# Layer 3's attention: probabilities turned in 32x32 blocks by VectorE, values weighted in 32x32 tiles of TensorE, and the steps of layers 2 and 3 ordered anew

## What is computed

```python
q = (x @ Wq + bq).reshape(b, l, KVH, GROUPS, HD).transpose(0, 2, 3, 1, 4)   # KVH 8, GROUPS 4, HD 16
k = (ctx @ Wk + bk).reshape(b, s, KVH, HD).transpose(0, 2, 1, 3)
v = (ctx @ Wv + bv).reshape(b, s, KVH, HD).transpose(0, 2, 1, 3)
attn = softmax(einsum('bkgld,bksd->bkgls', q, k) / 4 + mask)
out = einsum('bkgls,bksd->bkgld', attn, v).transpose(0, 3, 1, 2, 4).reshape(b, l, H)
x = out @ Wo + bo + x;  return layer_norm(x) * gamma + beta
```

## Time and profile before

| | |
|---|---|
| median of 3 runs | 2371.73 us |
| the profiled execution's own time | 2371.22 us |
| its span | 2369.4 us |
| mean granted TensorE clock in it | 0.969 |
| layers 2 and 3 | about 1190 us to the end |

### The profile page before, as it was taken

How to read it: one execution, slowest core, us unless ns; L and a number is a source line. 1 busy time by engine, 2 the same in 40 slices (tenths; PEclk the granted TensorE clock), 3 DMA queues, 4 the chain that set the end, 5 groups by cost and what they waited for, 6 DMA issues and landing times. The chain is left out here.

```text
span 2369.4 us, 56637 instructions
## 1 busy us (share of the span) xinstructions
PE 2177.4 (92%) x22208; PEld 1581.3 (67%) x22208; DVE 1132.9 (48%) x3132; ACT 1166.2 (49%) x3500; POOL 567.6 (24%) x573
## 2 busy tenths in 40 slices
...
GB/s 161 174 103 60 53 57 56 56 56 56 56 56 56 55 54 54 56 56 42 107 117 21 22 21 22 26 22 26 21 21 26 16 26 22 26 22 17 23 19 10
DMA packets 157658, 115.51 MB, mean 49 GB/s; under 512 B 87328, under 2 KB 132768, under 8 KB 155168
## 3 DMA queue, kind: packets, MB, share of 16 engines
...
## 5 line engine op out<-in xcount | busy, mean ns | idle before, releaser
L744 PE MATMUL bank<-normedT,mlp_w 128*128 128x128 f32 x2048 | 242.5, 278 | 18.3 <-ACT geluT L849 17.6
L744 PEld LDWEIGHTS bank<-normedT,mlp_w 128*128 128x128 f32 x2048 | 233.8, 193 | 31.4 <-ACT geluT L849 20.4
L754 PE MATMUL bank<-mlp_w,geluT 128*128 128x512 f32 x512 | 222.4, 592 | 0.0
L1970 ACT ACTIVATE scores<-scores,nmax 128x128 f32<-128x128 f32 x512 | 198.3, 396 | 2.5 <-DVE nmax L2232 2.5
L1458 POOL TENSOR_TENSOR k_even_odd<-k_even_odd,decay_products 128x512 f32<-128x512 f32 x80 | 98.3, 1228 | 327.1 <-PE quad L1654 251.5
L754 PEld LDWEIGHTS bank<-mlp_w,geluT 128*128 128x128 f32 x512 | 96.1, 190 | 114.8 <-issue 114.8
L857 ACT ACTIVATE probs<-probs,nmax 128x256 f32<-128x256 f32 x256 | 126.7, 496 | 26.3 <-DVE nmax L923 25.9
L1386 POOL TENSOR_TENSOR gn_rstd<-gn_var_eps,halfs 128x32 f32<-128x32 f32 x16 | 87.0, 5436 | 170.1 <-DVE gn_var_eps L2155 170.1
L2232 DVE CUSTOM_DVE_ANT_0 scores<-quad,mask 128x128 f32<-128x128 f32 x512 | 110.9, 286 | 32.0 <-PE quad L1773 32.0
L2120 DVE TENSOR_TENSOR rT<-rT,decay_products 128x256 f32<-128x256 f32 x96 | 40.9, 426 | 175.7 <-PE quad L1654 71.7
L923 DVE CUSTOM_DVE_ANT_0 probs<-quad,neg_mask 128x256 f32<-128x256 f32 x256 | 90.8, 420 | 71.1 <-PE quad L697 71.1
...
## 6 DMA issues: line engine op xcount, KB each, us to landing
probsT<-probs_turned_blocks SPq DMA_DIRECT2D x512, 64.0 KB, 2.0
...
```

The lines of the kernel that those rows point to most:

```text
L744: mm = nc.tensor.matmul(PS[b][:, f * P:(f + 1) * P], mlp_w1[:, c, m * P:(m + 1) * P], nT[:, c, :], start=(c == 0), stop=(c == NC - 1))
L754: mm = nc.tensor.matmul(PS[M.bank][:, :], gT[:, f, :], mlp_w2[:, f, :], start=(f == 0), stop=(f == NF - 1))
L1970: ac = nc.scalar.activation(s, s, ACT.Exp, bias=nmax[:, k, 2 * c + e:2 * c + e + 1], scale=-1.0, accum_out=rsum[:, kv, gr:gr + 1])
```

## The change

Scores are kept in one tile `sc` of nine slots of 512 columns. `prob(k, c, e)` spreads the 128 key tokens of a head over four slots, 32 tokens in each. `a_turn` moves from TensorE and ScalarE to VectorE: eight transposes in 32x32 blocks, each from slot k+1 into slot k. Since these turn blocks only, token groups end up on row groups; so the values are needed on all four: `a_vst` (ScalarE's queue) stores `v3` to DRAM, `a_rep` (SP) loads it back four times as `vrep`, so that each row group holds the values of all four groups of 32 tokens. `a_value` is one step of 128 products in 32x32 tiles (row group q, column group r) with 128 columns each, into the four banks of `quad`, and `a_norm` on VectorE reads these. Bank 4 joins the shared banks, and `ORDER` and `USES` are made anew for all stages. In `USES` (not shown below) only bank numbers differ, besides the turns that go and `a_value` that comes.

```diff
-        sc = [sb(f"scores{u}", [P, 2, 2, P]) for u in range(NU)]
-        scT = [sb(f"probsT3_{q}", [P, 2, 2, P]) for q in range(RG)]
+        sc = sb("scores3_turned", [P, 2 * RG + 1, D])
+        vrep = sb("v3_repeated", [P, RG, RG, 2, SB])
...
-        attn = sc[0][:, :, :, :].rearrange("p a e q -> p (a e) q")
-        rrep = sc[1][:, :, :, :].rearrange("p a e q -> p (a e q)")
-        y = sc[2][:, :, :, :].rearrange("p a e q -> p (a e q)")
+        attn = sb("attn3", [P, NC, P])
+        rrep, y, out = sc[:, 8, :], sc[:, 5, :], sc[:, 6, :]
+        v3_out = nc.dram_tensor("v3_blocks", (2, P, RG * 2 * SB), F32, kind="Internal").ap()
...
         ORDER = dict(
-            pe=[("p_t5",), ("a_x",), ("w_var",), ("p_t5t",), ("b_out",), ("p_mix",), ("a_q",), ("a_kv",), ("p_mix4",), ("p_k",),
-                ("w_rstd",), ("a_score", 0), ("p_u1",), ("p_r",), ("a_score", 1), ("p_w",), ("w_out",), ("a_turn", 0), ("p_level",
-                0), ("p_g",), ("a_turn", 2), ("p_level", 1), ("w_xc",), ("p_v",), ("a_turn", 3), ("p_level", 2), ("a_turn", 1),
-                ("n_xa",), ("w_fr",), ("p_level", 3), ("w_fk",), ("p_level", 4), ("a_turn", 4), ("a_value", 0), ("a_turn", 7),
-                ("a_turn", 5), ("p_level", 5), ("a_turn", 6), ("w_fv",), ("p_level", 6), ("a_norm",), ("a_value", 1), ("p_s0",),
-                ("p_av",), ("p_av6",)],
-            act=[("p_t5",), ("a_x",), ("p_t5t",), ("p_xm", 0), ("p_xm", 1), ("p_xm", 3), ("p_xm", 2), ("a_q",), ("a_kv",), ("p_xm",
-                 4), ("b_store",), ("p_k",), ("w_rstd",), ("p_u1",), ("a_exp", 0), ("p_r",), ("a_exp", 2), ("p_w",), ("a_exp", 3),
-                 ("a_exp", 1), ("p_g",), ("a_turn", 0), ("a_turn", 2), ("w_xc",), ("p_v",), ("a_turn", 3), ("a_exp", 6), ("n_xa",),
-                 ("a_exp", 4), ("a_turn", 1), ("a_exp", 7), ("w_fr",), ("a_exp", 5), ("w_fk",), ("a_turn", 4), ("a_turn", 7),
-                 ("a_turn", 6), ("a_turn", 5), ("p_level6",), ("a_norm",), ("a_bias",), ("p_wkv",)],
-            dve=[("n_ln1",), ("w_var",), ("b_out",), ("p_xm", 0), ("p_s0c",), ("p_xm", 3), ("p_xm", 1), ("b_ln",), ("p_xm", 4),
-                 ("w_rstd",), ("a_max", 0), ("a_max", 2), ("a_max", 1), ("a_max", 3), ("p_xm", 2), ("w_gate",), ("a_max", 6),
-                 ("a_max", 5), ("a_max", 4), ("a_max", 7), ("p_rup", 0), ("w_out",), ("p_merge", 0), ("n_nx",), ("w_ln2",),
-                 ("p_gate",), ("p_merge", 1), ("p_rup", 1), ("w_sx",), ("w_xr",), ("w_xk",), ("p_merge", 2), ("p_rup", 2), ("p_rup",
-                 3), ("p_merge", 3), ("n_shift",), ("a_rinv",), ("p_rup", 4), ("p_merge", 4), ("p_rup", 5), ("p_merge", 5),
-                 ("p_rup", 6), ("w_fv",), ("a_norm",)],
-            pool=[("w_pow",), ("b_rstd",), ("p_xm", 0), ("w_rep",), ("n_rstd",), ("p_xm", 3), ("n_first",), ("p_xm", 1), ("p_xm",
-                  4), ("p_k0",), ("a_x3b",), ("w_first",), ("p_xm", 2), ("p_ur",), ("p_wl",), ("p_kup", 0), ("w_rstd2",), ("p_kup",
-                  1), ("p_kup", 2), ("p_kup", 3), ("p_s0b",), ("p_kup", 4), ("a_norm",), ("p_kup", 5)],
-            sp=[("n_ldx",), ("w_lda",), ("n_lds0",), ("p_v",), ("p_ldw",)])
+            pe=[("p_t5",), ("a_kv",), ("p_t5t",), ("w_var",), ("p_mix",), ("a_x",), ("b_out",), ("a_q",), ("p_mix4",), ("p_k",),
+                ("w_rstd",), ("a_score", 0), ("p_u1",), ("p_r",), ("a_score", 1), ("p_w",), ("w_out",), ("p_level", 0), ("p_g",),
+                ("p_level", 1), ("w_xc",), ("p_v",), ("p_level", 2), ("n_xa",), ("p_level", 3), ("w_fk",), ("p_level", 4),
+                ("w_fr",), ("p_level", 5), ("w_fv",), ("p_level", 6), ("a_norm",), ("p_s0",), ("a_value",), ("p_av",), ("p_av6",)],
+            act=[("p_t5",), ("p_t5t",), ("a_kv",), ("p_xm", 0), ("a_x",), ("a_vst",), ("p_xm", 2), ("p_xm", 3), ("p_xm", 1),
+                 ("p_xm", 4), ("a_q",), ("p_k",), ("b_store",), ("w_rstd",), ("p_u1",), ("a_exp", 1), ("p_r",), ("p_w",), ("a_exp",
+                 0), ("a_exp", 2), ("a_exp", 3), ("a_exp", 5), ("w_xc",), ("p_v",), ("p_g",), ("a_exp", 4), ("a_exp", 7), ("a_exp",
+                 6), ("n_xa",), ("w_fk",), ("w_fr",), ("p_level6",), ("a_norm",), ("a_bias",), ("p_wkv",)],
+            dve=[("w_var",), ("n_ln1",), ("p_xm", 0), ("b_out",), ("p_xm", 3), ("p_s0c",), ("p_xm", 1), ("p_xm", 2), ("b_ln",),
+                 ("p_xm", 4), ("w_rstd",), ("a_max", 1), ("a_max", 0), ("a_max", 3), ("a_max", 2), ("w_gate",), ("n_nx",), ("a_max",
+                 5), ("a_max", 4), ("a_max", 6), ("a_max", 7), ("p_rup", 0), ("w_out",), ("p_merge", 0), ("a_turn", 0), ("w_ln2",),
+                 ("a_turn", 1), ("p_merge", 1), ("p_rup", 1), ("a_turn", 2), ("w_sx",), ("p_rup", 2), ("p_merge", 2), ("w_xk",),
+                 ("w_xr",), ("a_turn", 3), ("p_merge", 3), ("p_rup", 3), ("a_turn", 4), ("a_turn", 5), ("p_merge", 4), ("a_rinv",),
+                 ("p_rup", 4), ("a_turn", 6), ("p_gate",), ("p_rup", 5), ("p_merge", 5), ("a_turn", 7), ("p_rup", 6), ("n_shift",),
+                 ("w_fv",), ("a_norm",)],
+            pool=[("w_pow",), ("p_xm", 0), ("b_rstd",), ("w_rep",), ("p_xm", 1), ("p_xm", 3), ("w_first",), ("p_s0b",), ("n_rstd",),
+                  ("p_xm", 4), ("p_k0",), ("p_ur",), ("p_wl",), ("a_x3b",), ("p_kup", 0), ("w_rstd2",), ("p_xm", 2), ("n_first",),
+                  ("p_kup", 1), ("p_kup", 2), ("p_kup", 3), ("p_kup", 4), ("p_kup", 5), ("a_norm",)],
+            sp=[("w_lda",), ("a_rep",), ("p_v",), ("n_ldx",), ("p_ldw",), ("n_lds0",)])
...
+        def prob(k, c, e):
+            at = 256 * e + 64 * (k % RG) + SB * c
+            return sc[:, RG * (k // RG) + 1:RG * (k // RG) + 1 + RG, at:at + SB]
...
+                def a_rep(i, uses):
+                    sp.wait_ge(s_vst[i % 2], 16 * (i // 2 + 1))
+                    if later(i):
+                        u = uses[("a_value",)]
+                        sp.wait_ge(u.ready, u.made - 1)
+                    for q in range(RG):
+                        sp.dma_start(vrep[SB * q:SB * q + SB, :, :, :, :].rearrange("j m r e d -> j m (r e d)"),
+                                     v3_out[i % 2].rearrange("(m j) n -> j m n", m=RG)).then_inc(s_rep, 16)
...
                 def a_norm(i, uses):
-                    u = uses[("a_turn", 1)]
-                    pool.wait_ge(u.ready, u.made)
+                    pool.wait_ge(s_turned, NU * (i + 1))
...
-                def a_turn(i, uses, k):
-                    pe.wait_ge(s_exp, NU * i + rank("act", "a_exp", k) + 1)
-                    turn4(uses[("a_turn", k)], BANK["a_turn", k], sc[k][:, :, :, :].rearrange("p a e q -> p (a e q)"))
-                def a_value(i, uses, half):
-                    if half == 0 and later(i):
-                        pe.wait_ge(s_attn, i)
-                    for t in latest([uses[("a_turn", RG * half + r)] for r in range(RG)]):
-                        pe.wait_ge(t.free, t.done)
-                    for e in range(2):
-                        for r in range(RG):
-                            mm = nc.tensor.matmul(PS[OAV][SB * r:SB * r + SB, half * 256:(half + 1) * 256], v3[:, r, e, :],
-                                                  scT[r][:, :, e, :], start=(e == 0), stop=(e == 1))
-                    mm.then_inc(s_av, 1)
+                def a_value(i, uses):
+                    u = uses[("a_value",)]
+                    claim(u)
+                    pe.wait_ge(s_turned, NU * (i + 1))
+                    pe.wait_ge(s_rep, 16 * RG * (i + 1))
+                    for m in range(RG):
+                        for e in range(2):
+                            for r in range(RG):
+                                for q in range(RG):
+                                    rr, at = slice(SB * q, SB * q + SB), 256 * e + 64 * r
+                                    mm = nc.tensor.matmul(PS[q][SB * r:SB * r + SB, 0:P], vrep[rr, m, r, e, :],
+                                                          sc[rr, m:2 * RG:RG, at:at + 64], start=(m == 0 and e == 0),
+                                                          stop=(m == RG - 1 and e == 1))
+                    mm.then_inc(u.ready, 1)
...
+                    if later(i):
+                        act.wait_ge(s_vst[(i - 1) % 2], 16 * ((i - 1) // 2 + 1))
                     nc.scalar.activation(v3[:, :, 0, 0:D3], vals[:, :, 0, :], ACT.Copy)
                     nc.scalar.activation(v3[:, :, 1, D3:SB], vals[:, :, 1, :], ACT.Copy).then_inc(u.free, 1)
+                def a_vst(i, uses):
+                    u = uses[("a_kv",)]
+                    act.wait_ge(u.free, u.done)
+                    if i > 1:
+                        act.wait_ge(s_rep, 16 * RG * (i - 1))
+                    act.dma_start(v3_out[i % 2], v3[:, :, :, :].rearrange("p r e d -> p (r e d)")).then_inc(s_vst[i % 2], 16)
...
-                            s = sc[k][:, c, e, :]
+                            s = prob(k, c, e)
...
-                def a_turn(i, uses, k):
-                    u = uses[("a_turn", k)]
-                    act.wait_ge(u.ready, u.made)
```

(65 more changed lines are left out.)

7 lines of the change are left out of this document (2 added, 5 removed).

## The result

The change makes the kernel slower: 2499.9 us median against 2371.1 us (four runs of each kernel), ratio 1.054 with a 95% interval of 1.051 to 1.056. The forecast was 2361 us, with a range up to 2392.

A forecast was written before the change was run, and what follows sets the result against it. TensorE was taken as the bound: a turn of 61.97 + 2.4 (a_value) + 1.3 (wait) + 1.8 (clock) = 67.5 us against 68.17, 0.7 less over 14 turns, so 2361 us; range for 8 in 10, 2336 to 2392.

The forecast's parts named there:

- What bounds the kernel, and what goes: Loop turn: TensorE's work sets its 68.17 us; removing a_turn (4.20) and two a_value steps leaves 61.97; other engines cost nothing.
- The wait ahead of level 3: Recurrence on TensorE: with w_fr moved, only n_xa covers the gap from level 2; 1.3 us new wait each turn.
- Its clock: TensorE behind the wait ahead of level 3: slower clock costs 1.8 us a turn, ends 0 and 3.2.
- rival (b): Behind the wait ahead of level 3: clock stays down twice as long, turn 68.9 us, 2381 us; chance 0.15.
- if the spread values were late, `a_value` would wait, at the very end of the turn; they have about 30 us: DMA loads a_rep ahead of a_value: about 30 us of time to arrive, so no cost counted.
- the signs of being wrong: Unnamed waits that would refute the forecast: on V spread by DMA, the scores' ninth slot, or in front of a_score 1.
- 2.4 us for `a_value`: New a_value step on TensorE: 128 tiled products, 256 records, taken at 2.4 us; ends 1.7 and 6.9.
- The 9.3 ns: Price per record for a_value, taken from p_level 4: 128 records of 32x32 tiles in 1.19 us.
- 61.97: Loop turn in us on TensorE without the removed steps: 68.17 - 6.20, before anything added.
- Rival (c): a_value: tiled products don't overlap as hoped, 144 ns per four tiles, 4.6 us; turn 69.7, 2392 us; chance 0.16.
- the likeliest case's own range: Whole kernel: 2350 to 2371 us, from 1.7 to 2.9 for a_value, 1.3 to 2.0 for the clock, +-3 at the ends.
- The Trainium skill's floor of about 25 ns: a_value: matmul starts never closer than about 25 ns would make 256 records 6.4 us; the forecast set this aside.

The follow-up runs named there:

- e3: Changed kernel with a_rep waiting for this turn's a_score 1, and parts of p_g and p_v moved to later gaps between levels: 2384.1 us, ratio 1.0064.
- e4: e3 with each a_value product taking 64 of its 128 columns, half of the weighted values left out: 2390.5 us in one run.

## Why the prediction was wrong

- **What bounds the kernel, and what goes: right.** With both waits away (e3) TensorE waits for no other engine in the loop, and its clock is 1.00. VectorE's transposes, ScalarE's copies and the strided `a_max` stand behind no wait in the list, as forecast.
- **The wait ahead of level 3: right**, 1.1 us for 1.3. **Its clock: somewhat undersized**, 2.5 us on average over the loop (level 3 2.6 us from start to start and `w_fk` 5.6, for 1.92 and 3.77) against the 1.8 taken. The turn shown has 3.2 (2.86 and 6.04), the end that rival (b) had. Together 3.6 us a turn for 3.1.
- **A step that failed: "if the spread values were late, `a_value` would wait, at the very end of the turn; they have about 30 us".** I put the loads behind `w_lda` alone and read `u.made - 1` as the last turn's `a_value`. The semaphore belongs to the bank, and the count before `a_value`'s is `p_level` 6. The loads had no 30 us but the 1.7 us of `a_norm` and `p_s0`, against 4.5 from the first issue to the last landing. Cost: 61 us of the 129, some 38 of it the wait itself (13 times 2.9) and the rest in a slower `a_value` and the steps behind it. No rival held it; the signs of being wrong named it, a wait "on V spread by DMA".
- **The term that failed, and cost the most: 2.4 us for `a_value`.** At full clock its records come in 1.6 us per 128 (1.88 less the last record's own 0.27), 12.7 ns each, so 3.2 us. The 9.3 ns were taken from `p_level` 4, whose 64 products have 16 columns each; e4 has 9.9 ns with 64 columns. So the price was taken without its columns. With the pauses the step takes 4.9 to 7.6 us in e3, 5.4 on average. A row with 256 instructions in 1.2 us said nothing about 512 in a row: the price of a burst isn't its rate times its length. In e3 the pauses reach into `p_av` and `p_av6` too. Together the turn of e3 is 69.5 us where the sum without a wait gives 64.4 (61.97 + 2.4). Rival (c) had the size, 4.6 us, and mostly the wrong cause: by it the records would flow 36 ns apart (144 for four), and they flow at 12.7.
- **What each cost**, an estimate over 14 turns against the forecast of 2361 us: 61 us for the late load, 14 x 5.1 = 71 for `a_value` and its pauses, 14 x 0.5 = 7 for the clock behind level 3. That makes 139, which is also what 2499.9 lies over the forecast.
- **A slip in the likeliest case's own range:** its terms at their low ends (1.7 and 1.3 us) give a turn of 66.3 us and 2345, less 3 at the ends, not 2350.
- **The sum again** for the turn shown, from `a_kv` at 1699.79 to `a_kv` at 1778.89, 79.1 us: 61.97, + 10.9 (`a_value` with its wait), + 1.1, + 3.2, + 1.2 (`p_av` and `p_av6` at 1.2 GHz) = 78.4; 0.7 is left in small pieces. The mean turn grew by 128.8 / 14 = 9.2 us.
- The Trainium skill's floor of about 25 ns between matmul starts (TensorE: Matmul & The Clock Gate, Part 1), by which `a_value` would have been 6.4 us, doesn't hold for the new step either: 12.7 ns a record. Its 6.4 us lie near the length with the pauses, 5.4 on average in e3, by luck: the pauses have another cause.
